# GpSimd forms the weights of hop 1's late sums, and a group of sums stands behind every stage of its last softmax

## The chip, the cores and the metric

The kernel runs on one core of one Trainium2 chip. The metric is the device time of one execution in microseconds; of a kernel the median of its runs counts.

## What is computed

A graph network with three hops over 25,000 edges, sorted by their head node, and 50,000 nodes of 128 numbers. Cut to what matters:

```python
h = maximum(layernorm(x), 0)                # 50000 x 128
agg = h
for _ in range(3):
    hd, t = agg[head], agg[tail]            # 25000 x 128
    att = sum((hd @ q_w) * tanh((rel * t) @ k_w), axis=1)
    w = softmax of att over the edges with the same head
    summed = segment_sum(w[:, None] * rel * t, head)
    agg = summed / max(count(head), 1)
    agg = agg / max(norm(agg), 1e-12)
    out = out + agg + h
result = x + out
```

## The kernel before, in words

The edges lie in 200 tiles of 125; four tiles make a group, 50 groups in all, and these fall into four chunks of 13, 13, 13 and 11 groups (`GC`). A hop goes over the groups in steps. In each step GpSimd has gathered the tail rows (L611), VectorE multiplies them with the relations (L1109), TensorE turns them (L1407), multiplies with the two matrices (L1414, L1427 or L1429), ScalarE takes the tanh (L1258), and VectorE forms the scores (L1133).

When all scores of a chunk are there, its **softmax** runs in eight stages (`softmax`, L961). VectorE and TensorE take turns: VectorE scans along rows and asks (`ask`), TensorE transposes (L1445, L1388, L1389, L1394, L1400) and answers. Stage 3 hands the differences to ScalarE for the exponential. Stage 7 leaves the weights of the chunk's edges in `wcol`, and `wfl` with the edges that belong to segments running over the end of a tile.

A **group of sums** (`sums`, L1079 on VectorE, L1471 on TensorE, L1279 on ScalarE) is this chain. VectorE forms four tiles of weights, `wr = (segbc == lcol) * wcol`, one instruction of 128x125 per tile (`weights`, L1040, L1047), in a ring of two groups: a group may be formed when TensorE has finished the group before the last (`s_T`). TensorE multiplies each with the tile's rows into one of two PSUM banks (L1478), once ScalarE has emptied that bank (`s_nr`). ScalarE forms the squares' sums (L1289) and copies the group back to `rt` (L1291). After VectorE has formed the weights of group j, it scales group j - 6 (`scale`, L1067), and at every fifth group first forms the scales of five groups from the squares' sums (`norms`, L1055 to L1062, twelve small instructions). SP then stores the scaled group (L506).

A segment that runs over a tile's end needs carries. TensorE forms two **partial sums** per tile (`parts`, L1461), VectorE scans them (`carries`, L1017), TensorE turns the result (L1468), VectorE copies it to `fxr` (L1038), and SP moves it into two rows of `rt` (L491). The first group of the next chunk waits for that (`s_cy`).

Most groups of the first three chunks are summed within the steps of the hop (`sums_by_step`). Those left over come after the last step, and this is where the change lies. In hop 1 these are groups 28 to 38 (`sums_left`), with the last chunk's softmax, its partial sums and its own groups 39 to 49. The order before, in hop 1:

- stages 0 to 4, with one of groups 28 to 32 behind each (`FILL = 5`, `sum_behind`); then stages 5, 6, 7 with none
- the 44 tiles of partial sums of the last chunk in four lots of 11, with one of groups 33 to 36 behind each (`sums_mixed`, `parts_left`)
- the carries, then groups 37 and 38 (`HOLD = 2`), then 39 to 49

After that come the last scales and stores. GpSimd's first gather of hop 2 waits for all stores of hop 1 (`s_cs`). In hops 0 and 2, 25 groups are left over.

Each engine works its queue in order, so an instruction of the softmax that stands behind a group of sums on TensorE waits for that group's weights too.

GpSimd's queue is: the gathers of hop 0 (L611), the scatter of its sums (L623), the 200 gathers of hop 1, the wait for hop 1's stores, the 200 gathers of hop 2, the scatter to the output. Its waits go through a helper (`pool_wait`, L594) that also counts up a semaphore of its own.

Of the kernel before, what the change touches and what calls it, by code (L numbers as in the profile page):

```python
# [9 lines left out]
ALU = mybir.AluOpType  # L10
# [4 lines left out]
R = 125  # L15
# [4 lines left out]
GT = 4  # L20
NG = NT // GT
# [4 lines left out]
K = 4  # L26
GC = [0, 13, 26, 39, NG]
# [90 lines left out]

FILL, HOLD = 5, 2

def sums_left(h):
    return range(SUMS[h][-1].stop, GC[LAST])

def sums_mixed(h):
    return sums_left(h)[FILL:len(sums_left(h)) - HOLD]

def sums_held(h):
# [2 lines left out]

def sum_behind(h, i):

    return sums_left(h)[i:i + 1] if i < FILL else range(0)

def parts_left(h, j):

    mixed = sums_mixed(h)
    each = -(-CT[LAST] // len(mixed))
    n = j - mixed.start
    return range(min(n * each, CT[LAST]), min((n + 1) * each, CT[LAST]))

def gnn_kernel(nc, x, src, dst, etype, edge_emb, q_w, k_w, out):
    ctx = ExitStack()  # L150
    with ctx:
        def sb(name, shape, dt=F32):
            return ctx.enter_context(nc.sbuf_tensor(name, shape, dt))

        def sem(name):
            return ctx.enter_context(nc.semaphore(name))
# [16 lines left out]
        segbc = sb("segbc", [P, NT, R], U8)  # L173
# [6 lines left out]
        wr = sb("wr", [P, 2 * GT, D])  # L180
# [26 lines left out]
        lcol = sb("lcol", [P, NT])  # L207
# [8 lines left out]
        wcol = sb("wcol", [P, NT])  # L216
# [114 lines left out]
        s_wf = sem("s_wf")  # L331
# [23 lines left out]
        s_w = sem("s_w")  # L355
        s_T = sem("s_T")
# [234 lines left out]
        def _(pool):  # L591
            G = nc.gpsimd

            def pool_wait(sem_, value):  # L594
                pool.wait_ge(sem_, value)
                pool.sem_inc(s_pace, 1)
# [13 lines left out]
            def fetch(row, n, table, idx, done):  # L610
                G.indirect_dma_start(out=row, out_offset=None, in_=table[:, :],  # L611
                                     in_offset=bass.IndirectOffsetOnAxis(ap=idx[:, n:n + 1], axis=0)).then_inc(done, 16)
# [39 lines left out]
            for g in range(NG):  # L652
                if g >= TS:
                    pool_wait(s_rt, NG + g - TS + 1)
                for t in range(GT):
                    fetch(tr[:, (g % TS) * GT + t, :], g * GT + t, ntab_d, tidx, s_t[g % TS])

            pool_wait(s_cs, 2 * 16 * NG)
            for g in range(NG):  # L660
# [12 lines left out]
        def _(dve):  # L673
# [366 lines left out]
            def weights(h, j):  # L1040
                if h == 0 and j == 0:
                    dve.wait_ge(s_bc, 16)
                if j >= 2:
                    dve.wait_ge(s_T, h * NG + j - 1)
                for t in range(GT):
                    n = j * GT + t
                    ins = V.tensor_scalar(wr[:, (j % 2) * GT + t, 0:R], segbc[:, n, :], lcol[:, n:n + 1], wcol[:, n:n + 1],  # L1047
                                          ALU.is_equal, ALU.mult)
                ins.then_inc(s_w, 1)

            def norms(h, i):

                dve.wait_ge(s_nr, h * NG + NB * (i + 1))
                v, y, a, z = (nwt[0:R, k, :] for k in range(4))
                ch(V.tensor_scalar(v, ssq[0:R, i % 2, :], 1e-30, None, ALU.max))  # L1055
                ch(V.tensor_scalar(y.bitcast(I32), v.bitcast(I32), -0.5, RSQRT_BITS, ALU.mult, ALU.add))
                for k in range(3):
                    ch(V.scalar_tensor_tensor(a, y, -0.5, y, ALU.mult, ALU.mult))
                    ch(V.tensor_tensor(a, a, v, ALU.mult))
                    ch(V.scalar_tensor_tensor(z, a, 1.5, y, ALU.add, ALU.mult))  # L1060
                    y, z = z, y
                ch(V.scalar_tensor_tensor(nsc[0:R, :], y, 1e12, invc[0:R, i * NB * GT:(i + 1) * NB * GT], ALU.min, ALU.mult))  # L1062

            def scale(h, j):
                u = j % NB
                if h < HOPS - 1:
                    V.tensor_tensor(edge_rows(j)[0:R], edge_rows(j)[0:R],  # L1067
                                    nsc[0:R, u * GT:(u + 1) * GT].unsqueeze(2).to_broadcast([R, GT, D]), ALU.mult).then_inc(s_ag, 1)
                    return
                dve.wait_ge(s_fl[j % 2], 48 * (j // 2 + 1))  # L1070
                for t in range(GT):
                    n = j * GT + t
                    ch.note(V.scalar_tensor_tensor(rt[0:R, n, 0:D], rt[0:R, n, 0:D], nsc[0:R, u * GT + t:u * GT + t + 1],  # L1073
                                                   base_in[j % 2][0:R, t, :], ALU.mult, ALU.add))
                ch.join()
                ch(V.tensor_tensor(edge_rows(j)[0:R], edge_rows(j)[0:R], one_in[j % 2][0:R], ALU.add))  # L1076
                V.tensor_tensor(edge_rows(j)[0:R], edge_rows(j)[0:R], two_in[j % 2][0:R], ALU.add).then_inc(s_ag, 1)

            def sums(h, j):  # L1079
                weights(h, j)  # L1080
                if j >= LAG:
                    if (j - LAG) % NB == 0:
                        norms(h, (j - LAG) // NB)
                    scale(h, j - LAG)
# [56 lines left out]
            for h in range(HOPS):  # L1141
                for s in range(STEPS[h]):
                    if h == 0:
# [14 lines left out]
                        for i, g in enumerate(unit):  # L1158
                            dve.wait_ge(s_t[g % TS], t_value(0, g))
                            for t in range(GT):  # L1160
                                j = (g % TS) * GT + t
# [33 lines left out]
                for j in sums_mixed(h):  # L1195
                    sums(h, j)
# [357 lines left out]
```

## Time and profile before

| what | value |
|---|---|
| median of 3 runs | 1969.43 us (1954.67 to 1972.27) |
| profiled execution | 1960.66 us, span 1958.8 us |
| granted TensorE clock, mean | 0.698 |
| PE busy | 1080.3 us (55%) |
| DVE busy | 1314.4 us (67%) |
| ACT busy | 859.3 us (44%) |
| POOL busy | 1260.1 us (64%) |
| weights on DVE (L1047), 600 instructions | 168.4 us |
| PE idle before L1478, ended by those weights | 111.0 us |

### The profile page before, as it was taken

How to read it: one execution, taken by the hardware profiler on the slowest of the kernel's cores; microseconds unless marked ns; L12 is line 12 of the kernel's file. 1: busy time of each engine (PE TensorE's matmuls, PEld its weight loads, DVE VectorE, ACT ScalarE, POOL GpSimd, SP SyncE). 2: the span in 40 equal slices, each digit the busy share in tenths (PEclk: the TensorE clock that was granted, in tenths of full speed). 3: DMA queues.
4: the chain of work that ended last, by engine and by line, in shares of the span. 5: the costliest groups of instructions: out<-in, count | busy, mean ns of one | idle time of the engine just before them, and what ended most of it. 6: DMA issues, size and time to landing. Idle time of an engine off the chain costs nothing. (4 is left out here: it accounts for less than half of the span.)

```text
span 1958.8 us, 23309 instructions
## 1 busy us (share of the span) xinstructions
PE 1080.3 (55%) x5196; PEld 861.5 (44%) x5196; DVE 1314.4 (67%) x5817; ACT 859.3 (44%) x2657; POOL 1260.1 (64%) x1218
## 2 busy tenths in 40 slices
PE   0112454458678587940016688787366886956410
PEld 0102333337456465930014567577244674746410
DVE  8896788786676675789813556865535458599870
ACT  3331666666564644656622243553422233234420
POOL 1005777667777777778777777700277777667776
PEclk9999866565676665565557887985677888655555
DMA  8925555554433334346745555621477789567761
GB/s 228 247 62 192 176 183 180 174 169 150 120 100 108 112 115 154 131 145 220 255 147 139 159 150 153 182 87 56 134 152 157 152 169 179 136 173 217 216 190 34
DMA packets 196490, 303.96 MB, mean 155 GB/s; under 512 B 31344, under 2 KB 113596, under 8 KB 189824
## 3 DMA queue, kind: packets, MB, share of 16 engines
q1 hardware_dynamic: 157952, 229.50, 36.6%
q0 software_dynamic: 38400, 72.99, 17.9%
q8 instruction: 42, 0.69, 0.1%
q14 instruction: 96, 0.79, 0.1%
HBM read 176.41 MB, written 131.38 MB: 157 GB/s over the span
## 5 line engine op out<-in xcount | busy, mean ns | idle before, releaser
L611 POOL DMA_INDIRECT tr<-in_x_dram,tidx x200 | 213.8, 1069 | 233.3 <-DVEq L845 152.1
L1478 PE MATMUL ps<-rt,wr 128*125 128x128 f32 x1200 | 256.6, 382 | 128.7 <-DVE wr L1047 111.0
L611 POOL DMA_INDIRECT tr<-agg_d,tidx x200 | 199.0, 995 | 191.0 <-issue 189.8
L1407 PE MATMUL ps<-ident,rt 128*128 128x128 f32 x600 | 133.7, 363 | 295.0 <-DVE rt L1109 177.8
L1478 PEld LDWEIGHTS ps<-rt,wr 128*125 128x125 f32 x1200 | 223.8, 278 | 148.7 <-DVE wr L1047 130.1
L1289 ACT ACTIVATE sqj<-ps,invc 125x128 bf16<-125x128 f32 x600 | 212.4, 374 | 171.3 <-PE ps L1478 171.3
L1252 ACT COPY turns<-ps 128x512 f32<-128x512 f32 x150 | 87.7, 585 | 411.5 <-PE ps L1407 407.1
L623 POOL DMA_INDIRECT ntab_d<-rt,lidx x200 | 224.0, 1120 | 63.9 <-issue 60.2
L623 POOL DMA_INDIRECT out_dram<-rt,lidx x200 | 211.3, 1056 | 73.6 <-issue 59.7
L611 POOL DMA_INDIRECT tr<-ntab_d,tidx x200 | 201.8, 1009 | 67.1 <-issue 62.6
L611 POOL DMA_INDIRECT xr<-in_x_dram,hidx x200 | 202.7, 1013 | 61.0 <-issue 59.5
L1414 PE MATMUL ps<-turns,kw 128*128 128x512 f32 x300 | 235.9, 881 | 8.7 <-ACT turns L1252 8.7
L1407 PEld LDWEIGHTS ps<-ident,rt 128*128 128x128 f32 x600 | 92.2, 186 | 322.1 <-DVE rt L1109 197.4
L1109 DVE TENSOR_TENSOR rt<-tr,relr 128x512 f32<-128x512 f32 x150 | 103.1, 688 | 147.7 <-DMA tr<-agg_d,tidx 86.7
L1461 PEld LDWEIGHTS ps<-wfl,rt 128*128 128x128 f32 x1200 | 189.9, 249 | 0.5
L1461 PE MATMUL ps<-wfl,rt 128*128 128x2 f32 x1200 | 186.0, 287 | 0.0
L1047 DVE TENSOR_SCALAR wr<-segbc,lcol,wcol 128x125 f32<-128x125 uint8 x600 | 168.4, 356 | 21.7 <-PE ps L1478 17.7
L1258 ACT ACTIVATE turns<-ps 128x512 f32<-128x512 f32 x150 | 89.6, 597 | 134.6 <-PE ps L1414 134.4
L1427 PEld LDWEIGHTS ps<-qwT,turns 128*128 128x128 f32 x624 | 107.2, 240 | 56.6 <-issue 55.0
L1289 ACT ACTIVATION_READ_ACCUMULATOR sqj<-ps,invc 125x1 f32 x600 | 127.9, 213 | 0.0
L1429 PEld LDWEIGHTS ps<-qwT,turns 128*128 128x128 f32 x576 | 99.2, 255 | 49.5 <-issue 40.6
L1133 DVE SCALAR_TENSOR_TENSOR junk<-ps,xr 128x128 bf16<-128x128 f32 x400 | 96.5, 282 | 25.2 <-PE ps L1429 24.2
(234 smaller groups left out, 2225.2 us busy)
## 6 DMA issues: line engine op xcount, KB each, us to landing
agg_d<-rt SPq DMA_DIRECT2D x100, 258.0 KB
xr<-agg_d SPq DMA_DIRECT2D x100, 258.0 KB, 3.3
relr<-rel_d SPq DMA_DIRECT2D x100, 256.0 KB, 3.9
ntab_d<-rt SPq DMA_DIRECT2D x15, 1679.7 KB
rt<-in_x_dram SPq DMA_DIRECT2D x13, 1024.0 KB, 6.7
out_dram<-rt SPq DMA_DIRECT2D x13, 1024.0 KB, 4.1
acc_d<-xr SPq DMA_DIRECT2D x50, 258.0 KB, 3.5
rel_d<-relr SPq DMA_DIRECT2D x50, 256.0 KB, 3.2
```

Of the source, the lines that this page charges most:

```text
L611: G.indirect_dma_start(out=row, out_offset=None, in_=table[:, :], in_offset=bass.IndirectOffsetOnAxis(ap=idx[:, n:n + 1], axis=0)).then_in ...
L623: G.indirect_dma_start(out=table[:, :], out_offset=bass.IndirectOffsetOnAxis(ap=lidx[:, n:n + 1], axis=0), in_=rt[:, n, 0:width], in_offse ...
L1047: ins = V.tensor_scalar(wr[:, (j % 2) * GT + t, 0:R], segbc[:, n, :], lcol[:, n:n + 1], wcol[:, n:n + 1], ALU.is_equal, ALU.mult)
L1109: V.tensor_tensor(edge_rows(g), ring(tr, g, TS), ring(relr, g, RS), ALU.mult).then_inc(s_rt, 1)
L1133: ins = V.scalar_tensor_tensor(junk[:, t, :], z, 1.0, left[:, (g % n) * GT + t, 0:D], ALU.mult, ALU.mult, accum_out=att[:, g * GT + t:g * ...
L1289: A.activation(sqj[0:R, t, :], ps[B_T + j % 2][0:R, t, :], ACT.Square, scale=invc[0:R, n:n + 1], accum_out=ssq[0:R, j // NB % 2, k:k + 1]) ...
L1407: ins = T.transpose(ps[B_TR][:, t, :], rt[:, g * GT + t, 0:D], ident[:, :])
L1414: T.matmul(bank(B_KW), kw[:, :], flat2(rtT[:, (g % 2) * GT:(g % 2 + 1) * GT, :]), start=True, stop=True).then_inc(s_rg, 1)
L1427: ins = T.matmul(z, th, qwT[:, :], start=True, stop=True)
L1429: ins = T.matmul(ps[B_Z + g % 2][:, t, :], th, qwT[:, 0:D], start=True, stop=True)
L1461: ins = T.matmul(bank(B_S)[:, 2 * n:2 * n + 2], rt[:, TC[b] + n, 0:D], wfl[:, n, :], start=True, stop=True)
L1478: ins = T.matmul(ps[B_T + j % 2][0:R, t, :], wr[:, (j % 2) * GT + t, 0:R], rt[:, j * GT + t, 0:D], start=True, stop=True)
```

## The change

In hop 1, from group 28 on, GpSimd forms the weights (22 groups, 88 instructions), and VectorE leaves them out. `FILL` becomes a list: in hop 1 there is now a group of sums behind each of the eight stages (28 to 35). That leaves one group, 36, among the partial sums, so all 44 stand in one block ahead of it. Groups 37 to 49 are as before. Hops 0 and 2 keep their order, and their weights stay on VectorE.

```diff
-FILL, HOLD = 5, 2
+FILL, HOLD = [5, 8, 5], 2
...
 def sums_mixed(h):
-    return sums_left(h)[FILL:len(sums_left(h)) - HOLD]
+    return sums_left(h)[FILL[h]:len(sums_left(h)) - HOLD]
...
 def sum_behind(h, i):
-    return sums_left(h)[i:i + 1] if i < FILL else range(0)
+    return sums_left(h)[i:i + 1] if i < FILL[h] else range(0)
+
+
+def by_pool(h, j):
+
+    return h == 1 and j >= sums_left(h)[0]
...
             for g in range(NG):
                 if g >= TS:
                     pool_wait(s_rt, NG + g - TS + 1)
                 for t in range(GT):
                     fetch(tr[:, (g % TS) * GT + t, :], g * GT + t, ntab_d, tidx, s_t[g % TS])
 
+            pool_wait(s_w, NG + sums_left(1)[0])
+            for j in range(sums_left(1)[0], NG):
+                if j == sums_left(1)[0] or j in GC:
+                    pool_wait(s_wf, K + 1 + max(c for c in range(K) if GC[c] <= j))
+                pool_wait(s_T, NG + j - 1)
+                for t in range(GT):
+                    n = j * GT + t
+                    ins = G.tensor_scalar(wr[:, (j % 2) * GT + t, 0:R], segbc[:, n, :], lcol[:, n:n + 1], wcol[:, n:n + 1],
+                                          ALU.is_equal, ALU.mult)
+                ins.then_inc(s_w, 1)
+
             pool_wait(s_cs, 2 * 16 * NG)
...
             def sums(h, j):
-                weights(h, j)
+                if not by_pool(h, j):
+                    weights(h, j)
                 if j >= LAG:
```

`s_wf` counts the chunks whose softmax is done, and `s_w` the groups of weights formed.

TensorE, hop 1, from stage 5 to the carries, before (L1394 is stage 5, L1400 stage 6, L1461 the partial sums, L1478 groups of sums, x4 each):

```order
L1394 MATMUL ps<-ident,rcar 44x1 x2
L1400 MATMUL ps<-ident,wlin 128x44
L1459 MATMUL ps<-cell,onesr 128x1
L1461 MATMUL ps<-wfl,rt 128x2 x11
L1478 MATMUL ps<-rt,wr 125x128 x4
L1461 MATMUL ps<-wfl,rt 128x2 x11
L1478 MATMUL ps<-rt,wr 125x128 x4
L1461 MATMUL ps<-wfl,rt 128x2 x11
L1478 MATMUL ps<-rt,wr 125x128 x4
L1461 MATMUL ps<-wfl,rt 128x2 x11
L1478 MATMUL ps<-rt,wr 125x128 x4
L1468 MATMUL ps<-ident,cT 44x128 x2
```

The same stretch now (L1412 is stage 5, L1418 stage 6, L1479 the partial sums, L1496 groups of sums):

```order
L1412 MATMUL ps<-ident,rcar 44x1 x2
L1496 MATMUL ps<-rt,wr 125x128 x4
L1418 MATMUL ps<-ident,wlin 128x44
L1496 MATMUL ps<-rt,wr 125x128 x8
L1477 MATMUL ps<-cell,onesr 128x1
L1479 MATMUL ps<-wfl,rt 128x2 x44
L1496 MATMUL ps<-rt,wr 125x128 x4
L1486 MATMUL ps<-ident,cT 44x128 x2
```

Three groups of sums have moved ahead: one behind stage 5, and two (x8) behind stage 6 and stage 7, which gives TensorE nothing to do. The 44 tiles of partial sums stand together, with one group between them and the carries' transposes (L1486).

VectorE, hop 1, from the carries' copy (L1038) on, before (L1047 weights, L1067 the scaling of a group, L1055 to L1062 the scales of five groups):

```order
L1038 COPY fxr<-ps 44x256
L1047 TENSOR_SCALAR wr<-segbc,lcol,wcol 128x125 x4
L1067 TENSOR_TENSOR rt<-rt,nsc 125x4x128
L1047 TENSOR_SCALAR wr<-segbc,lcol,wcol 128x125 x4
L1067 TENSOR_TENSOR rt<-rt,nsc 125x4x128
L1047 TENSOR_SCALAR wr<-segbc,lcol,wcol 128x125 x4
L1067 TENSOR_TENSOR rt<-rt,nsc 125x4x128
L1047 TENSOR_SCALAR wr<-segbc,lcol,wcol 128x125 x4
L1067 TENSOR_TENSOR rt<-rt,nsc 125x4x128
L1047 TENSOR_SCALAR wr<-segbc,lcol,wcol 128x125 x4
L1055 TENSOR_SCALAR nwt<-ssq 125x20
L1056 TENSOR_SCALAR nwt<-nwt 125x20
```

The same place now (L1055 the copy, L1084 the scaling, L1072 on the scales):

```order
L1055 COPY fxr<-ps 44x256
L1084 TENSOR_TENSOR rt<-rt,nsc 125x4x128 x4
L1072 TENSOR_SCALAR nwt<-ssq 125x20
L1073 TENSOR_SCALAR nwt<-nwt 125x20
L1075 SCALAR_TENSOR_TENSOR nwt<-nwt 125x20
L1076 TENSOR_TENSOR nwt<-nwt 125x20
```

The weights of groups 37 to 41 are gone from between the scalings. GpSimd's queue shows where they went; before:

```order
L623 DMA ntab_d<-rt,lidx 50000x129 x32
L616 IOTA rt 128x100
L623 DMA ntab_d<-rt,lidx 50000x129 x168
L611 DMA tr<-ntab_d,tidx 128x129 x200
L611 DMA tr<-agg_d,tidx 128x129 x200
L623 DMA out_dram<-rt,lidx 50000x128 x200
```

and now:

```order
L629 DMA ntab_d<-rt,lidx 50000x129 x32
L622 IOTA rt 128x100
L629 DMA ntab_d<-rt,lidx 50000x129 x168
L617 DMA tr<-ntab_d,tidx 128x129 x200
L671 TENSOR_SCALAR wr<-segbc,lcol,wcol 128x125 x88
L617 DMA tr<-agg_d,tidx 128x129 x200
L629 DMA out_dram<-rt,lidx 50000x128 x200
```

The 88 instructions stand between the last gather of hop 1 (L617) and the first of hop 2. No other engine's queue has anything added; ScalarE and SP keep their order.

## Rows read from the trace of the kernel before

**Rows 1.** windows: stages, partial sums, tail and end of hop 1

```profile
core 0: us, PE busy (x) PEld busy (x) DVE busy (x) ACT busy (x) POOL busy (x), PEclk, DMA share, GB/s
1313.10:1335.40 22.30, 12.22 (x53) 9.71 (x51) 19.28 (x80) 12.12 (x56) 0.00 (x0) 0.50 0.18 70
1335.40:1362.30 26.90, 26.88 (x124) 26.34 (x124) 9.76 (x38) 6.33 (x30) 0.00 (x0) 0.50 0.11 40
1362.30:1396.30 34.00, 20.39 (x104) 18.32 (x104) 26.79 (x91) 26.50 (x125) 0.00 (x0) 0.74 0.29 111
1396.30:1406.10 9.80, 2.03 (x8) 1.86 (x8) 6.20 (x23) 0.02 (x1) 0.00 (x0) 0.55 0.37 136
```

**Rows 2.** chain that ended last, same part: start us, us, what

```profile
1313.21 1.11 DVE wr L1047 x4
...
1327.94 1.12 DVE wr L1047 x4
...
1335.41 0.58 PE ps L1459 x2
1335.99 4.79 PE ps L1461 x22
1340.78 1.91 PE ps L1478 x8
...
1361.87 0.44 PE ps L1468 x2
...
1362.75 1.03 DVE wr L1047 x4
```

**Rows 3.** timeline of the stages: start us, us, engine, line, [idle before <-releaser]

```profile
1314.38 2.07 PE L1478 MATMUL ps<-rt,wr 128*125 128x128 f32 x8 [0.60 <-DVE wr L1047]
...
1331.37 0.15 DVE L934 TENSOR_TENSOR seg_xf<-seg_x,ps 44x1 f32<-44x1 f32 x1 [1.05 <-PE ps L1394]
...
1334.43 0.33 PE L1400 MATMUL ps<-ident,wlin 44*128 44x44 f32 x1 [3.10 <-DVEq L820]
```

**Rows 4.** timeline of the tail of hop 1

```profile
1376.44 3.69 PE L1478 MATMUL ps<-rt,wr 128*125 128x128 f32 x16 [3.09 <-DVE wr L1047]
...
1378.29 0.37 ACT L1289 ACTIVATE sqj<-ps,invc 125x128 bf16<-125x128 f32 x1 [2.44 <-PE ps L1478]
...
1390.48 0.37 ACT L1289 ACTIVATE sqj<-ps,invc 125x128 bf16<-125x128 f32 x1 [2.69 <-PE ps L1478]
...
1396.36 0.18 DVE L1055 TENSOR_SCALAR nwt<-ssq 125x20 f32<-125x20 f32 x1 [3.56 <-ACT rt L1291]
```

**Rows 5.** chain, tail and end of hop 1: squares, copy, store

```profile
1365.93 1.50 ACT sqj L1289 x8
1367.43 0.48 ACT rt L1291
...
1402.03 3.01 DMA agg_d<-rt
```

**Rows 6.** timeline, carries of chunk 2: from their copy to the sum behind them

```profile
1302.71 0.42 DVE L1038 COPY fxr<-ps 52x256 f32<-52x256 f32 x1 [2.27 <-PE ps L1468]
...
1307.11 0.95 PEld L1478 LDWEIGHTS ps<-rt,wr 128*125 128x125 f32 x8 [0.22 <-DMA rt<-fxr]
```

**Rows 7.** groups on POOL: xcount | busy us, mean ns | idle before

```profile
L611 POOL DMA_INDIRECT tr<-agg_d,tidx x200 | 199.0, 995 | 191.0 <-issue 189.8 <-DVE rt L1109 1.2
L604 POOL IOTA rt<- 128x256 f32 x7 | 5.0, 739 | 0.0
...
L616 POOL IOTA rt<- 128x100 f32 x2 | 0.7, 373 | 0.0
L601 POOL TENSOR_SCALAR_AFFINE_SELECT ident<-ident 128x128 f32<-128x128 f32 x1 | 0.3, 292 | 0.1
```

**Rows 8.** groups by form, 1286 to 1402 us, scaling on DVE

```profile
L1067 DVE TENSOR_TENSOR rt<-rt,nsc 125x512 f32<-125x512 f32 x32 | 21.5, 684 | 0.2
```

**Rows 9.** chain in hop 2: 26 instructions of partial sums

```profile
1598.70 2.80 PE ps L1461 x26
```

## The prediction

> **What bounds the kernel now.** I read the page first (no engine is busy for the whole span), then the chain that ended last, then the waits and the timeline of the one place that the change touches: the last part of hop 1, from the moment the last scores are formed (1313.1 us) to the first gather of hop 2 (1406.1). Everything of hop 2 waits for the stores at its end, so what this part gives is given to the span. The windows [rows 1] cut it in four. In all of them GpSimd has 0.00 to 0.02 us of work.
>
> - Stages, 22.3 us. The last softmax is a ladder between VectorE and TensorE. Five of its eight stages have a group of sums behind them, and the chain runs over the four weights of each on VectorE, 1.11 us per group (first and last of five in [rows 2]). TensorE is busy for 12.22 of 22.30 us at a granted clock of 0.50, which is its 1.2 GHz level. It stood idle for 0.60 us for the first weights and for 3.10 us ahead of stage 6's transpose; VectorE waited 1.05 us behind a group of sums [rows 3].
> - Partial sums, 26.9 us: TensorE is full (26.88) and the chain stays on it [rows 1, 2]: 22 instructions of partial sums, a group of sums at 1.91 us, four times over.
> - Tail, 34.0 us, thirteen groups (37 to 49). ScalarE does 26.50 us of work, VectorE 26.79. After every five groups VectorE forms the scales, and weights stand in its queue behind that; TensorE then stands for 3.09 us for weights, and ScalarE for 2.44 and 2.69 us [rows 4].
> - End: scales, five groups scaled, the last store of 3.01 us [rows 5].
>
> **The change, part by part.** The sum is made against the profiled execution, 1960.66 us (span 1958.8); the median of the runs shown is 1969.43, so that execution lies 8.8 us below it.
>
> *The weights leave VectorE.* 22 groups (28 to 49), 88 instructions, about 1.1 us a group, 24 us of VectorE's time. The same 88 go to GpSimd, which has nothing to do there, behind the 200 gathers of hop 1 and ahead of the wait for the stores, and that wait ends later anyway. The trace has none of these on GpSimd, so their price is bounded. From below: of the ops it does show, the affine_select over 128 elements took 0.292 us, the iotas 0.373 for 100 elements and 0.739 for 256, that is 2.35 ns per element and 0.14 us fixed [rows 7]; 125 elements would be 0.43 by that. The far upper end is the one other GpSimd instruction, the gather's, at 0.995. I take 0.4 (between the two near rows), 1.6 us a group; with a wait ahead of it, some 1.8.
>
> *What stands in GpSimd's way.* Before each group it waits until TensorE has finished the group before the last (two buffers of weights). A buffer's round is then 1.8 + 2.07 (TensorE, low clock, [rows 3]) + 0.2 that I allow for signalling = 4.1 us for two groups, 2.03 each. ScalarE needs 1.50 + 0.48 [rows 5] and 0.12 that I allow between groups, 2.1 each. So GpSimd is just not the bound, at 0.4 us an instruction. Behind its waits nothing else is queued until the gathers of hop 2.
>
> *Stages.* I walked the ladder with the weights ready in time and TensorE at its low clock. TensorE's queue keeps its order, so each stage's transposes come behind a 2.07 us group. Group 28 then runs from 1313.8 (1314.38 in [rows 3]), 29 from 1316.2, 30 and 31 from 1318.6 to 1322.7, 32 from 1325.3 (ahead of it VectorE forms the scales of five groups, as before), 33 to 1329.8. Stage 6 is asked at about 1330.6 instead of 1334.4, since the weights no longer lie between the stages. Group 34 runs to 1333.1 and 35 to 1335.2; VectorE is done with stage 7 by 1332. TensorE has room: 12.22 + 3 x 2.07 = 18.4 of 22.3 us. The partial sums then start where they do now, 1335.4. Cost of three more groups in the stages: 0. If that cover failed wholly it would be 6.2.
>
> *Partial sums.* Three of the four groups between them are gone to the stages: 3 x 1.91 = 5.7 us less, and 44 partial sums in one block keep their 18.2 us (the stretch from 1335.99 to 1361.87 less four groups of 1.91). TensorE comes to the carries' transposes at 1356.1 instead of 1361.87. **Gain 5.7.**
>
> *Tail.* Group 37's weights no longer wait for the carries' copy on VectorE (1362.75 in [rows 2]), and there is no stall at the scales. What is late next is ScalarE: 2.1 us for the first group on TensorE, 13 x 2.1 = 27.3, and 0.6 because group 39 needs the carries' rows landed: copy to sum took 4.4 us in [rows 6], while TensorE would get there 0.6 sooner. Together 30.0 instead of 34.0. **Gain 4.0.** The end (last scales, five groups scaled, store) is the same.
>
> *A shared port.* In this stretch GpSimd and VectorE never worked at once [rows 1], so no row shows what they do to each other. Some 20 instructions of the ladder have two inputs in SBUF, and so has each scaling, 0.684 us [rows 8]. Bounds: 0, and a full GpSimd instruction of 0.4 ahead of each of the 20, 8 us. GpSimd is at work about two thirds of the time and a wait is on average half an instruction, but in the stages TensorE's groups cover most of it. I take **1.2 lost**. (The Trainium skill, SBUF — State Buffer, section Who interferes with whom, speaks against the change here: a VectorE instruction with two SBUF inputs and a GpSimd instruction that reads SBUF exclude each other, and the later one blocks fully. By it the term is above zero; no run here shows it yet.)
>
> Sum: 5.7 + 4.0 - 1.2 = 8.5 us. 1960.66 - 8.5 = 1952.2; from the median, 1969.43 - 8.5 = **1960.9 us**, 0.4% less.
>
> **Rivals.**
>
> *A. GpSimd just becomes the bound.* With 0.7 us an instruction a group takes 2.8 us, more than ScalarE's 2.1. Group 28's weights, begun once VectorE has formed group 27's (before the 1313.21 of [rows 2]), stand at about 1314.4, as now [rows 3]; group 35's, seven times 2.8 later, at 1334, so the stages end a microsecond later. The block of partial sums gives its 5.7. In the tail group 38's weights wait for group 36, and eleven groups at 2.8 eat most of the gain: in all about 2 us faster, 1967.4. For it: the iota's row at 256 elements costs 0.739. Against: 125 elements are half of that. (The Trainium skill, GPSIMD Engine Reference, section Elementwise — side-by-side cycle accounting, gives about 2.6 cycles an element against VectorE's one, and calls it roughly twice as slow; 125 elements at 2.6 cycles of 1.2 GHz is 0.27 us before dispatch, an estimate. Twice VectorE's time would be this rival.)
>
> *B. GpSimd is far too slow (slower than before).* At 1.0 us an instruction, the gather's price, a group needs 4.2 us with its wait. TensorE's queue holds each stage's transposes behind a group without weights: group 35's weights stand at 1345 (28's at 1315.8, then seven times 4.2), so the partial sums start at 1347 instead of 1335.4; they and group 36 end at 1368; groups 38 to 49 then come every 4.2 us, and ScalarE ends at about 1422 instead of 1396.3. That is 26 us slower, 1995. It decides from about 0.72 us an instruction (slower at all), and passes 1% from about 0.93. For it: nothing on this engine shows float compare and multiply from bytes. Against: its near rows are all under 0.43 at this size.
>
> *C. TensorE's clock rises.* The stages and the partial sums run at 0.50 now [rows 1]; in the tail it is 0.74. With groups back to back in the stages it may stand at its 2.4 GHz level when the partial sums start. At that level 26 instructions took 2.80 us [rows 9], 44 partial sums (88 instructions) 9.5 instead of 18.2: 8.7 more, and up to 2 in the stages. Gain 17 to 19, 1951. For it: after a run of groups without a gap the tail's clock rises. Against: TensorE was full from 1335.4 to 1362.3 and its clock still stayed at 0.50, so partial sums alone do not raise it, nor perhaps hold it.
>
> *D. The stages give nothing back*, since the ladder itself gets longer by what leaves the partial sums: gain about 3, 1966.
>
> **Chances.** Forecast 0.52, A 0.14, B 0.10, C 0.16, D 0.08. The runs before spread from 1954.67 to 1972.27, so about 1% (20 us) is what a measurement can tell from no change. Range: C below with some spread, 1946; above, A and D with the spread of a median, and part of B, 1975; B's own time is left out with its 0.10. The forecast's own range is 1953 to 1968. Faster by over 1% needs C and luck: 0.13. Slower by over 1% is most of B: 0.08. Within: 0.79.
>
> **What would show it.** Right: 88 instructions of weights on GpSimd near 0.4 us each; the block of partial sums starting within 1.5 us of where it did and 18 us long; TensorE not waiting for GpSimd in the tail, ScalarE's groups 2.1 us apart; the carries 5 to 6 us sooner; first gather of hop 2 near 1397 to 1398 us. Wrong: TensorE's waits named after GpSimd's weights and groups further apart than 2.3 us (A, B); a granted clock above 0.6 in the partial sums (C); partial sums that start after 1338 (D); VectorE's scaling well over 0.684 us (the port's term); or a hop 2 whose length is not that of before by more than 3 us, where nothing is changed.

## The result and the profile after

| kernel | median | profiled execution | span |
|---|---|---|---|
| before | 1967.43 us (20 runs, 1954.67 to 1973.32) | 1960.66 us | 1958.8 us |
| after | 1978.7 us (20 runs, 1965.23 to 1994.05) | 1978.9 us | 1977.0 us |

The ratio is 1.0063, 95% interval 1.0043 to 1.0082: about 12.4 us slower. The forecast was 8.5 us faster, 1960.9, and its range ended at 1975.

Both traces are cut at the same five events: the transposes of the last scores, the first matmul of the partial sums' block, the carries' transposes, the end of ScalarE's last copy, and the first gather of hop 2.

| section, us | before | after | difference |
|---|---|---|---|
| stages of the last softmax | 22.05 | 29.40 | +7.35 |
| partial sums | 26.25 | 21.15 | -5.10 |
| tail | 34.66 | 47.50 | +12.84 |
| end | 9.80 | 9.60 | -0.20 |
| sum | 92.77 | 107.65 | +14.88 |

After came to the first event 2.1 us earlier (1311.28 against 1313.36), so its first gather of hop 2 stands at 1418.92 instead of 1406.12: 12.8 us later, close to the 12.4 of the ratio. The two spans differ by 5.4 us more, in hop 2, where nothing is changed; that part varied by more than 10 us between the executions below. Of the profiled executions below, those of experiments 2, 3 and 4 are over 1.5% longer than the fastest of the same kernel, so only their sections are compared, which repeat where nothing in them was changed.

The windows of after, cut like [rows 1] (us; PE, PEld, DVE, ACT and POOL busy with their instructions; granted clock; DMA share and GB/s):

```profile
core 0: us, PE busy (x) PEld busy (x) DVE busy (x) ACT busy (x) POOL busy (x), PEclk, DMA share, GB/s
1311.30:1340.70 29.40, 18.10 (x76) 14.84 (x74) 18.81 (x68) 16.26 (x74) 29.40 (x34) 0.50 0.20 78
1340.70:1361.80 21.10, 21.10 (x99) 21.06 (x99) 3.10 (x14) 1.98 (x9) 4.62 (x6) 0.50 0.04 13
1361.80:1409.30 47.50, 26.83 (x108) 22.90 (x105) 14.72 (x39) 27.74 (x126) 42.94 (x48) 0.54 0.21 80
1409.30:1418.90 9.60, 2.03 (x8) 1.86 (x8) 6.21 (x23) 0.02 (x1) 0.00 (x0) 0.50 0.37 138
```

POOL is busy for 29.40 of 29.40 us in the stages and for 42.94 of 47.50 in the tail. It is the engine that had nothing to do here before. VectorE, which the change was to relieve, is down to 14.72 us in the tail, and ScalarE, which the forecast saw as the next bound, works 27.74 of 47.50. The waits of after from 1300 to 1430 us (who waits <- for what: us in all, times, longest) say the same in one row each:

```profile
ACT sqj L1307 <- PE ps L1496: 54.3, 22, 19.3
...
DVE nwt L1072 <- ACT rt L1309: 35.0, 4, 10.9
PEld ps L1496 <- POOL wr L671: 32.7, 19, 3.7
PE ps L1496 <- POOL wr L671: 27.7, 19, 3.4
...
PE ps L1496 <- DVE wr L1064: 4.1, 2, 2.5
```

TensorE waited 19 times for GpSimd's weights, 27.7 us in all. The 54.3 us of ScalarE behind TensorE (39.9 in the same stretch before) are in part the same shortage one engine further on; a wait names only the engine just ahead. The timeline of the stages, which answers to [rows 3] (idle time and its releaser in brackets), shows how regular it is:

```profile
1313.99 2.07 PE L1496 MATMUL ps<-rt,wr 128*125 128x128 f32 x8 [2.29 <-POOL wr L671]
...
1317.29 2.07 PE L1496 MATMUL ps<-rt,wr 128*125 128x128 f32 x8 [1.00 <-POOL wr L671]
...
1324.21 2.07 PE L1496 MATMUL ps<-rt,wr 128*125 128x128 f32 x8 [1.03 <-POOL wr L671]
...
1328.33 2.07 PE L1496 MATMUL ps<-rt,wr 128*125 128x128 f32 x8 [1.14 <-POOL wr L671]
...
1338.68 2.07 PE L1496 MATMUL ps<-rt,wr 128*125 128x128 f32 x8 [1.40 <-POOL wr L671]
...
1341.19 18.93 PE L1479 MATMUL ps<-wfl,rt 128*128 128x2 f32 x88
```

Before, TensorE stood for 0.30 to 1.41 us for VectorE's weights ahead of each of five groups, 4.05 in all. Now it stands for GpSimd's ahead of each of eight, 2.29 at group 28 and 0.94 to 1.59 at the others, 10.4 in all, and the partial sums (last row) begin 29.9 us after the first event instead of 22.6. The tail, for [rows 4]:

```profile
1362.84 2.48 DVE L1084 TENSOR_TENSOR rt<-rt,nsc 125x512 f32<-125x512 f32 x4
...
1367.58 1.72 PE L1496 MATMUL ps<-rt,wr 128*125 128x128 f32 x8 [3.42 <-POOL wr L671]
...
1381.77 2.07 PE L1496 MATMUL ps<-rt,wr 128*125 128x128 f32 x8 [2.83 <-POOL wr L671]
...
1384.86 2.07 PE L1496 MATMUL ps<-rt,wr 128*125 128x128 f32 x8 [1.02 <-POOL wr L671]
...
1387.95 2.07 PE L1496 MATMUL ps<-rt,wr 128*125 128x128 f32 x8 [1.02 <-POOL wr L671]
...
1399.04 2.07 PE L1496 MATMUL ps<-rt,wr 128*125 128x128 f32 x8 [2.78 <-POOL wr L671]
...
1409.35 0.18 DVE L1072 TENSOR_SCALAR nwt<-ssq 125x20 f32<-125x20 f32 x1 [10.95 <-ACT rt L1309]
```

From the group at 1384.86 to that at 1387.95 it is 3.09 us: GpSimd's own pace, four instructions. The longer idle times (3.42, 2.83, 2.78) stand at groups 38, 42 and 47. 12 steps of 3.09, and 2.2, 1.8 and 1.8 more at the three long ones, make 42.9 us; the rest of 47.5 is 0.4 ahead of the first step and 4.2 for TensorE's and ScalarE's work on the last group.

The price of one instruction, which [rows 7] could only bound, is now a row of the page (xcount | busy, mean ns | idle before):

```profile
L671 POOL TENSOR_SCALAR wr<-segbc,lcol,wcol 128x125 f32<-128x125 uint8 x88 | 77.9, 900 | 53.5 <-DVE wr L1064 36.6
```

and by the view of that line alone (ns, least/median/most):

```profile
L671 POOL TENSOR_SCALAR wr<-segbc,lcol,wcol x88: 785/789/2969, 1310.3 to 1404.4; 128x125 f32<-128x125 uint8 x88
```

The median is 0.789 us where I took 0.4. The mean of 0.900 and the longest of 2.969 show a second thing, taken up below.

### The profile page after: what moved, and what is told of

It is laid out like the page before. It is cut to its first block and busy times, and to the rows that moved or that the text cites. A ratio compares the mean times of both kernels' runs of the same rounds, so it can differ in the third digit from the quotient of the medians.

```text
span 1977.0 us, 23334 instructions
## 1 busy us (share of the span) xinstructions
PE 1084.8 (55%) x5196; PEld 865.4 (44%) x5196; DVE 1295.4 (66%) x5729; ACT 861.3 (44%) x2657; POOL 1331.5 (67%) x1306
## 5 line engine op out<-in xcount | busy, mean ns | idle before, releaser
L617 POOL DMA_INDIRECT tr<-in_x_dram,tidx x200 | 211.3, 1057 | 230.9 <-DVEq L862 152.0
L1496 PE MATMUL ps<-rt,wr 128*125 128x128 f32 x1200 | 263.7, 389 | 139.7 <-DVE wr L1064 98.6
L1496 PEld LDWEIGHTS ps<-rt,wr 128*125 128x125 f32 x1200 | 228.9, 284 | 161.2 <-DVE wr L1064 110.8
L617 POOL DMA_INDIRECT tr<-ntab_d,tidx x200 | 200.2, 1001 | 72.9 <-issue 65.8
L617 POOL DMA_INDIRECT tr<-agg_d,tidx x200 | 197.4, 987 | 74.4 <-issue 59.8
L617 POOL DMA_INDIRECT xr<-in_x_dram,hidx x200 | 204.3, 1022 | 61.0 <-issue 59.4
L1479 PEld LDWEIGHTS ps<-wfl,rt 128*128 128x128 f32 x1200 | 188.4, 248 | 0.5
L1479 PE MATMUL ps<-wfl,rt 128*128 128x2 f32 x1200 | 185.4, 287 | 0.0
L1064 DVE TENSOR_SCALAR wr<-segbc,lcol,wcol 128x125 f32<-128x125 uint8 x512 | 143.8, 362 | 11.3 <-PE ps L1496 7.9
L671 POOL TENSOR_SCALAR wr<-segbc,lcol,wcol 128x125 f32<-128x125 uint8 x88 | 77.9, 900 | 53.5 <-DVE wr L1064 36.6
```

The costliest lines, as they stand in the source:

```text
L1479: ins = T.matmul(bank(B_S)[:, 2 * n:2 * n + 2], rt[:, TC[b] + n, 0:D], wfl[:, n, :], start=True, stop=True)
L1496: ins = T.matmul(ps[B_T + j % 2][0:R, t, :], wr[:, (j % 2) * GT + t, 0:R], rt[:, j * GT + t, 0:D], start=True, stop=True)
```

## The experiments

All are compared by the sections above. The sections hold no wait for a large transfer, and they came out alike where nothing in them was changed: the partial sums took 21.15 us in nine of the kernels below, and 26.25 in the three that keep their old order. The timing of a whole execution says less: it moves by several us in hop 2. The first four ran on a chip on which the kernel before itself took 2519.87 us, and transfers were slower there (119 to 123 GB/s over the span in these four profiles instead of 157); their ratios are 0.997 [0.989, 1.005], 0.999 [0.989, 1.009], 0.994 [0.986, 1.002] and 0.987 [0.978, 0.997]. These don't decide between theories a few us apart. The last of them even lies below 1 while its four sections are 1.2 us longer; what gave that kernel its time elsewhere is open.

| us | stages | partial sums | tail | end | sum |
|---|---|---|---|---|---|
| before | 22.05 | 26.25 | 34.66 | 9.80 | 92.77 |
| after | 29.40 | 21.15 | 47.50 | 9.60 | 107.65 |
| 1. order alone | 27.25 | 21.15 | 34.59 | 9.85 | 92.84 |
| 2. GpSimd alone, old order | 23.57 | 26.25 | 47.62 | 9.32 | 106.75 |
| 3. 32 columns | 22.74 | 21.15 | 34.35 | 9.28 | 87.54 |
| 4. GpSimd in the stages alone | 29.19 | 21.15 | 34.45 | 9.21 | 94.00 |
| 5. four columns | 21.88 | 18.04 | 31.09 | 9.07 | 80.08 |
| 6. constants | 23.57 | 21.15 | 36.88 | 9.10 | 90.70 |
| 7. short scalings | 27.16 | 21.15 | 43.07 | 9.13 | 100.52 |
| 8. seven groups on GpSimd | 24.20 | 21.15 | 30.33 | 9.14 | 84.82 |
| 9. three groups, old order | 22.10 | 26.25 | 28.75 | 9.25 | 86.35 |
| 10. 32 columns, short scalings | 20.59 | 21.15 | 28.43 | 8.81 | 78.97 |
| 11. float input | 29.13 | 21.15 | 47.43 | 9.56 | 107.28 |

Two theories stood at the start. GpSimd's price: an instruction costs about 0.79 us and nothing else matters much. Against it the order: eight groups among the stages hold the softmax up whoever forms their weights.

**1. The order alone.** VectorE forms all weights again, in the new order.

```diff
 def by_pool(h, j):
-    return h == 1 and j >= sums_left(h)[0]
+    return False
```

> The new order of groups alone: a group behind each of the eight stages, and all weights on VectorE. Theory 1 (the loss comes from GpSimd's 0.79 us an instruction, the order is sound): the stretch from the last score to the partial sums grows by 3 to 5 us against the kernel before (22.9 us there), the partial sums and group 36 take 20.3 us up to the carries' transposes instead of 26.3, the tail stays at 34 us; in all 1 to 3 us less than before, ratio about 0.999. Theory 2 (the order itself costs what the partial sums give, rival D): the stages grow by 6 us or more, ratio 1.000 to 1.002.

The result lies between the two theories: the stages grew by 5.2, and nothing is gained in all. The sum is that of before, 92.84 against 92.77. What leaves the partial sums (5.1 us) comes back in the stages (5.2): the ladder gets longer by VectorE's weights for three more groups. The tail is unchanged. Its timeline in the stages (this chip's times lie later; L1485 groups of sums, L1407 the transpose of stage 6):

```profile
1725.13 2.07 PE L1485 MATMUL ps<-rt,wr 128*125 128x128 f32 x8 [0.84 <-DVE wr L1053]
...
1742.77 0.33 PE L1407 MATMUL ps<-ident,wlin 44*128 44x44 f32 x1 [1.44 <-DVEq L826]
...
1743.97 4.16 PE L1485 MATMUL ps<-rt,wr 128*125 128x128 f32 x16 [0.87 <-DVE wr L1053]
```

TensorE waits for weights ahead of the groups (0.84, 0.87 us) and for VectorE's request ahead of the transpose (1.44 us): VectorE has both to do, one after the other, and the request comes later for each group of weights ahead of it. So the order alone is worth nothing, and costs nothing either. Of after's 7.35 us in the stages, 5.2 are there with VectorE's weights too, and GpSimd adds 2.15.

**2. GpSimd alone.** The old order, GpSimd's weights.

```diff
-FILL, HOLD = [5, 8, 5], 2
+FILL, HOLD = [5, 5, 5], 2
```

> The weights of hop 1 from group 28 on by GpSimd, in the old order (five stages with a group, four lots of partial sums). Theory 1: the tail is as long as in the changed kernel, 46 to 48 us instead of 34, since GpSimd forms a group in 3.1 us and more where a scaling of VectorE blocks it; the stages grow by 2 to 4 us; the lots of partial sums hide GpSimd. In all 14 to 17 us more than before, ratio about 1.008, a little worse than the changed kernel's 1.0063. Theory 2: ratio at or below 1.004, since three groups less in the stages wait for GpSimd.

The tail is as long as after's (47.62), the partial sums are as before, and the stages, with five groups instead of eight, take 23.57. The loss in the tail is GpSimd's alone. In the stages GpSimd alone costs 1.5 us (2 to 4 were expected), the order alone 5.2, and both together 7.35. The sum is 14.0 us longer than before, as expected; the ratio can't tell it on that chip.

**3. A shorter instruction.** GpSimd forms 32 of the 125 columns.

```diff
-G.tensor_scalar(wr[:, (j % 2) * GT + t, 0:R], segbc[:, n, :], ...
+G.tensor_scalar(wr[:, (j % 2) * GT + t, 0:32], segbc[:, n, 0:32], ...
```

> The changed kernel with GpSimd's instructions cut to 32 of 125 columns, so 93 columns of each tile's weights in hop 1 from group 28 on are left as they were and the sums there are not the reference's. This tells whether GpSimd's price is the one term that failed. Theory 1: an instruction falls to 0.2 to 0.35 us, GpSimd is no longer waited for, the partial sums start about where they do in the kernel before, the tail takes 29 to 31 us instead of 34: 6 to 10 us less than before, ratio 0.995 to 0.997, which is the forecast. Theory 2 (the price of an instruction is mostly fixed): it stays above 0.6 us and the ratio above 1.002. Theory 3 (my walk of the stages or the tail was wrong too): GpSimd is fast and the ratio still at 0.999 or above.

```profile
L671 POOL TENSOR_SCALAR wr<-segbc,lcol,wcol x88: 463/470/2975, 1749.3 to 1824.2; 128x32 f32<-128x32 uint8 x88
```

The median of 0.470 us lies between the first two theories (0.2 to 0.35, and over 0.6). At it the order does what the forecast said of it: 22.74 us of stages with eight groups, and the 5.1 us of the partial sums kept. But the tail is still 34.35, not 29 to 31. Four instructions at 0.47 are 1.9 us a group, no more than ScalarE needs, so a second cost was left in it: the longest instruction still took 2.975 us.

**4. GpSimd for groups 28 to 36 alone.**

```diff
-    return h == 1 and j >= sums_left(h)[0]
+    return h == 1 and sums_left(h)[0] <= j < 37
```

> The changed kernel with GpSimd for groups 28 to 36 alone; from group 37 on VectorE forms the weights as before. Theory 1: the tail goes back to 33 to 35 us and only the stages' loss against the partial sums' gain is left, about +2 us: ratio 1.000 to 1.002. Rival: the tail stays long (over 40 us), so that something else than the weights' maker lengthens it.

The tail goes back to 34.45, the stages stay at 29.19. Each loss is there without the other: 7.1 us here, 13.0 in the tail of experiment 2.

**5, 6, 11. What the price is made of.** Four columns instead of 125; constants in place of the two columns of scalars; a float tile (`ident`) as input in place of bytes.

```diff
-... segbc[:, n, :], lcol[:, n:n + 1], wcol[:, n:n + 1], ...
+... segbc[:, n, 0:4], lcol[:, n:n + 1], wcol[:, n:n + 1], ...   (5, output 0:4)
+... segbc[:, n, :], 3.0, 0.5, ...                               (6)
+... ident[:, 0:R], lcol[:, n:n + 1], wcol[:, n:n + 1], ...      (11)
```

> The changed kernel with GpSimd's instructions cut to 4 of 125 columns (121 columns of each tile's weights from group 28 of hop 1 on are left as they were). From 125 columns (0.773 us from start to start) and 32 columns (0.447) a line gives 0.335 us fixed and 3.5 ns a column. Theory: 0.35 us here. If it is 0.30 or less or 0.40 or more, the line does not hold and part of the price has another shape (steps, or a floor).

> The changed kernel with constants (3.0 and 0.5) in place of the two columns lcol and wcol that GpSimd's instruction reads per partition, so the sums from group 28 of hop 1 on are not the reference's. With 125 columns an instruction took 0.79 us and with 32 columns 0.60 on average, so the price is mostly fixed. Theory 1: the fixed part is the reading of the two scalar columns; then an instruction falls to 0.4 us or less, and the tail from 47.5 to about 34. Theory 2: the fixed part belongs to the instruction itself; then it stays at 0.7 us or more and the tail at 45 us or more.

> The changed kernel with GpSimd's instruction reading 125 float columns (the identity matrix) instead of 125 bytes of segbc, so the sums from group 28 of hop 1 on are not the reference's. Theory 1 (the 3.5 ns a column are the reading of bytes and their conversion): an instruction falls from 0.773 us, start to start, to 0.65 or less. Theory 2 (they are the two operations a column): it stays within 0.03 of 0.773, and the sections keep their lengths of 29.4, 21.2 and 47.5 us.

The same line of each trace, first with four columns:

```profile
L671 POOL TENSOR_SCALAR wr<-segbc,lcol,wcol x88: 372/378/2969, 1318.1 to 1386.5; 128x4 f32<-128x4 uint8 x88
```

with constants:

```profile
L671 POOL TENSOR_SCALAR wr<-segbc x88: 635/638/2991, 1314.2 to 1392.2; 128x125 f32<-128x125 uint8 x88
```

with float input:

```profile
L671 POOL TENSOR_SCALAR wr<-ident,lcol,wcol x88: 786/788/2968, 1309.1 to 1403.0; 128x125 f32<-128x125 f32 x88
```

From one start to the next, in a stretch without a wait, it is 0.773 us for 125 columns, 0.447 for 32 and 0.360 for 4. A line through the first two has 3.5 ns a column and 0.335 us fixed, and gives 0.349 for the third. Constants make it 0.606, between the two theories of experiment 6, and the tail 36.88. So the two columns of scalars cost 0.167 us of an instruction of 125 columns; whether that is fixed or grows with the columns no run shows. Bytes or floats make no difference (789 and 788). VectorE starts one of these every 0.254 us, four in 1.02, so GpSimd is 3.0 times as slow in this one. (The Trainium skill, GPSIMD Engine Reference, section Elementwise — side-by-side cycle accounting, has about 2.6 cycles an element and a ratio of 1.96, for an add of two tensors. This instruction, with one tensor and two columns of scalars, is dearer in the trace: 3.5 ns is 4.2 cycles at that section's 1.2 GHz, and the ratio is 3.0.)

**7. The shared port.** VectorE's scalings are cut to one of their four tiles (125x128 in place of 125x512) from group 22 on; they last 0.31 us on the mean instead of 0.72. The weights are full size.

```diff
+if h == 1 and j >= 22:
+    V.tensor_tensor(edge_rows(j)[0:R, 0:1], edge_rows(j)[0:R, 0:1], ...
+    return
```

> The changed kernel with VectorE's scaling cut to one of four tiles from group 22 of hop 1 on, so three quarters of those rows stay unscaled. It takes away most of the time in which VectorE reads two inputs in SBUF. Theory 1 (that is what stretches GpSimd's instructions beyond 0.79 us: 2.97 us for the one that meets four scalings in a row, 1.39 for each of three that meet a row of five): the longest falls below 1.3 us, the mean from 0.90 to about 0.82, and the tail from 47.5 to 43 or 44 us. Rival: the long ones stay, and the mean stays at 0.88 or more; then they belong to GpSimd itself.

```profile
L671 POOL TENSOR_SCALAR wr<-segbc,lcol,wcol x88: 786/789/1370, 1307.3 to 1394.7; 128x125 f32<-128x125 uint8 x88
```

The longest instruction falls from 2.969 to 1.370 us (below 1.3 was expected), the tail by 4.4 and the stages by 2.2. In the tail VectorE is idle most of the time, so its own shorter work cannot give that; it is what the scalings did to GpSimd. The 1.370 stands beside a row of four short scalings, so part of the cost is still there, and 4.4 is the least that the port takes in the tail. In the stages part of the 2.2 may be VectorE's own time. How it happens stands in after's timeline: the tail's first row above is four scalings back to back from 1362.84, 2.48 us. The GpSimd instruction that began at 1363.02, in the first of them, ended at 1365.98, 0.67 us behind the last. The two later sets of five scales free five scalings each, and GpSimd's group of that moment took 4.9 us instead of 3.1. There GpSimd wasn't kept out for the whole row: its instructions took 1.39 us three times at 1377.57, and 1.91 and 1.39 at 1395.70. VectorE pays less; by after's groups of 1286 to 1409 us:

```profile
L1084 DVE TENSOR_TENSOR rt<-rt,nsc 125x512 f32<-125x512 f32 x27 | 18.6, 719 | 1.0
...
L1077 DVE SCALAR_TENSOR_TENSOR nwt<-nwt 125x20 f32<-125x20 f32 x15 | 3.5, 234 | 0.5
```

The scaling is at 719 ns on the mean against 684 in [rows 8]. That mean mixes two kinds: 19 of the 27 took 674 to 694 ns, among them the four that kept GpSimd out, and eight took 760 to 934. The small instruction of the scales, L1077, is at 234 against 178 for the same one before. (The Trainium skill, SBUF — State Buffer, section Who interferes with whom, says that the two exclude each other and the later one is blocked fully. For GpSimd at 1363.02 the trace agrees, 2.97 us. For VectorE it doesn't agree: no scaling was held for as much as half of a GpSimd instruction, and the last section has VectorE instructions that ran at their own length inside one.)

**10. Both at once.** Edits 3 and 7 together: a lower price, and less of the port.

> 32 of 125 columns in GpSimd's instructions and VectorE's scaling cut to one of four tiles from group 22 of hop 1 on (93 columns of the weights are left as they were, three quarters of the rows unscaled). With 32 columns alone the tail took 34.4 us although a group cost GpSimd only 1.8 us. Theory (three runs of scalings, each of which holds one GpSimd instruction for 2 to 3 us, make that tail): the tail falls to 28 to 30 us, the end by 2 us since the scalings are short, and no GpSimd instruction is longer than 1.4 us. Rival (the walk of the tail is wrong, ScalarE and TensorE need more than 2.1 us a group between them): the tail stays at 32 us or more.

```profile
L671 POOL TENSOR_SCALAR wr<-segbc,lcol,wcol x88: 466/474/1377, 1312.4 to 1379.3; 128x32 f32<-128x32 uint8 x88
```

Its windows (stages, partial sums, tail):

```profile
1313.60:1334.10 20.50, 14.40 (x75) 12.02 (x73) 13.43 (x61) 15.82 (x74) 17.47 (x34) 0.75 0.28 107
1334.10:1355.30 21.20, 21.20 (x100) 21.09 (x100) 3.49 (x19) 2.05 (x10) 1.93 (x5) 0.50 0.04 13
1355.30:1383.70 28.40, 18.34 (x107) 15.80 (x105) 8.08 (x39) 26.76 (x126) 23.52 (x48) 0.80 0.36 133
```

20.59 and 28.43 us. Against experiment 3 the tail gives 5.9, so the port is the second cost there too. The stages give 2.15, but TensorE's granted clock in them is 0.75 here and 0.58 in experiment 3, so that part can be the clock's. The end fell by 1.0 us to 8.81 where 2 were expected. ScalarE is now busy for 26.76 of 28.40 us in the tail: the bound that the forecast named. This and experiment 3 leave most of the weights unformed, so they tell what the rest of the kernel allows and are no kernels to use. One timed run each: 1948.66 us for this, 1954.86 for four columns, 1984.11 for float input, beside 1977.74 for the kernel before; 1965.58 for constants and 1970.89 for short scalings, beside 1966.73.

**8 and 9. Give GpSimd what it has time for.** If 3.1 to 4.9 us is the price of a group, GpSimd can do one in several, ahead of time, in buffers of its own, while VectorE does the others. In 8 that is seven groups in the new order, in 9 three in the old one: 37, 42 and 47, those that stood right behind the scales of five groups on VectorE.

```diff
+PG = [29, 31, 33, 35, 37, 42, 47]      # 9: [37, 42, 47] and FILL 5
 def by_pool(h, j):
-    return h == 1 and j >= sums_left(h)[0]
+    return h == 1 and j in PG
...
+for i, j in enumerate(PG):
+    if i > 1:
+        pool_wait(s_T, NG + PG[i - 2] + 1)
+    ... wp[:, (i % 2) * GT + t, 0:R] ...
+    ins.then_inc(s_wp, 1)
```

> A version to beat both: the new order with a group behind each stage, GpSimd forming only groups 29, 31, 33, 35, 37, 42 and 47 of hop 1, in two buffers of its own (the idle one-hot buffer), VectorE the others. 3.2 us a group then has two groups' time in the stages, and the three in the tail are those that stand behind VectorE's five-group scales. Theory 1: stages 24 to 26 us, partial sums 21, tail 29.5 to 31.5 us (ScalarE's 2.1 a group), last score to first gather 84 to 87.5 us instead of 92.8, ratio about 0.997. Rival (VectorE itself is the bound in the tail): the tail stays at 33 us or more.

> The order of the kernel before, with GpSimd forming only groups 37, 42 and 47 of hop 1 in buffers of its own. Theory 1: stages 22.1 and partial sums 26.2 us as before, tail 29.5 to 31.5 instead of 34.7, ratio about 0.998. Rival: the tail stays at 33 us or more since VectorE's own work, 26.8 us of 34, and the exchange with ScalarE set it and not the weights behind the scales.

Windows of 8:

```profile
1318.10:1342.30 24.20, 14.76 (x76) 12.20 (x74) 22.02 (x82) 15.63 (x74) 10.71 (x12) 0.71 0.23 87
1342.30:1363.40 21.10, 21.10 (x99) 21.05 (x99) 4.17 (x19) 2.23 (x10) 3.17 (x4) 0.50 0.05 19
1363.40:1393.70 30.30, 21.07 (x108) 18.07 (x105) 23.67 (x79) 26.97 (x126) 5.17 (x4) 0.76 0.33 124
1393.70:1402.90 9.20, 2.03 (x8) 1.86 (x8) 6.21 (x23) 0.05 (x1) 0.01 (x1) 0.57 0.38 144
```

and of 9:

```profile
1315.90:1338.00 22.10, 12.01 (x52) 9.51 (x50) 19.18 (x80) 12.15 (x56) 0.00 (x0) 0.50 0.18 68
1338.00:1364.30 26.30, 26.26 (x123) 26.20 (x124) 9.85 (x38) 5.95 (x27) 4.36 (x4) 0.50 0.11 41
1364.30:1393.00 28.70, 17.76 (x107) 14.61 (x105) 23.74 (x79) 27.16 (x126) 5.86 (x4) 0.86 0.35 131
1393.00:1402.30 9.30, 2.03 (x8) 1.85 (x8) 6.21 (x23) 0.04 (x1) 0.01 (x1) 0.50 0.38 142
```

Both are faster than before, by little. 8: 1955.32 us (12 runs), ratio to before 0.9953 [0.9928, 0.9979]. 9: 1959.55 us (12 runs), 0.9963 [0.9933, 0.9993]. The intervals overlap and don't tell the two apart. By the sections they are 8.0 and 6.4 us shorter than before, 0.41% and 0.33%. POOL is busy for 5.17 and 5.86 us in the tail, where ScalarE is the bound (26.97 of 30.30, 27.16 of 28.70). Kernel 9, which moves three groups and keeps the order, takes 5.9 us off the tail; the seven of kernel 8 give 4.3 there and 5.1 in the partial sums, and pay 2.15 in the stages. What the buffers of their own give, and what the fewer groups, was not told apart. A combination (the new order with VectorE's scalings kept away from GpSimd's groups) was not tried.

## Why the prediction was wrong, by its steps

**The step that failed is the price of GpSimd's instruction, "I take 0.4".** It measured 0.79 at the median and 0.90 on the mean. The rows it was taken from were of other kinds: the iota reads nothing, and its line (0.14 us fixed, 2.35 ns an element) was short in both terms, against 0.335 and 3.5 here. The far bound of 0.995 held, and the truth lay nearer to it than to the two rows that I took for near. Nearness in shape (some 125 elements) was not nearness in kind (an input in SBUF and two columns of scalars).

**The shared port, 1.2 lost:** wrong in size and in form. Experiment 7 gives 6.7 us back (4.4 in the tail, 2.2 in the stages), within the bounds of 0 to 8; not the whole of it, since short scalings still hold GpSimd, and with some of VectorE's own time in it. I had priced the small instructions that wait for GpSimd. What cost was GpSimd held at rows of scalings, which the sum did not have.

**Stages, 0:** right for weights that come in time (22.74, 21.88 and 20.59 us in experiments 3, 5 and 10, against 22.05 before), wrong for those of after, +7.35. The text said that a failed cover would cost up to 6.2; the cover that failed was GpSimd's, which forms the eight groups in 28.3 us, 3.5 each, not TensorE's room (18.10 us busy, forecast 18.4). With VectorE's weights it fails too, by 5.2 (experiment 1).

**Partial sums, -5.7:** right, -5.10, at a clock of 0.50 as before; with the same block and other weights, experiments 1 and 3 have the same 21.15.

**Tail, -4.0 to 30.0:** the walk was right for its bound. With the bound really at ScalarE it took 28.43 (experiment 10), 28.75 (9) and 30.33 (8). With GpSimd at 3.1 us a group it took 47.50. **End, 0:** right, -0.20.

Put together, at the first gather of hop 2 the forecast was 21.3 us off (-8.5 against +12.8): 16.8 in the tail, 7.35 in the stages, 0.6 in the partial sums; less the 1.2 already taken for the port, the 2.1 of the earlier start and 0.2 at the end. Of the 24.2 in tail and stages experiment 7 gives 6.7 back; experiment 3, with the price at 0.47 and the scalings whole, gives 19.8 back, and both edits together 27.9, with a higher clock in the stages. So the price is the larger part; an exact split no run shows.

**Rivals.** B named what happened, with its place and its break-even: slower at all from 0.72 us, 1% slower from 0.93. Its own line (26 us at 1.0, nothing at 0.72) gives 5 us at 0.773 and 16 at 0.89, which is the pace in the tail with the port's share (42.9 us over 12 steps, a quarter of each); measured 12.8. It had a chance of 0.10 and was left out of the range. With a price bounded from 0.29 to 0.995 and a break-even at 0.72, nearly four tenths of those bounds lay beyond it, and the range should have reached some way into it. A was too mild: it put 0.7 on the near side. Its last sentence doesn't come out either: twice VectorE's 1.1 us a group is 2.2, 0.55 an instruction, which is near ScalarE's 2.1 a group and not A's 2.8. C did not happen in after (0.50 in stages and partial sums), but part of it is real. With four columns the three windows read:

```profile
1319.10:1340.90 21.80, 15.42 (x75) 13.08 (x73) 16.37 (x62) 15.52 (x74) 16.31 (x34) 0.66 0.27 104
1340.90:1359.00 18.10, 18.10 (x100) 17.98 (x100) 3.80 (x19) 2.31 (x10) 1.59 (x5) 0.59 0.04 16
1359.00:1390.10 31.10, 18.52 (x107) 16.07 (x105) 13.62 (x39) 27.09 (x126) 24.61 (x48) 0.83 0.33 121
```

The clock was granted at 0.66 in the stages and 0.59 in the partial sums, which took 18.04 us instead of 21.15. In experiment 10 it stood at 0.75 in the stages and 0.50 right behind them. D, the ladder that gets longer by what leaves the partial sums, is what experiment 1 shows, but with VectorE forming the weights, not GpSimd.

## What to carry to other kernels

Price an idle engine by an instruction of the same kind as the one it is to take, with the same inputs and scalars; if the trace has none, work out the price at which the change turns, and if that lies inside the bounds, let the range cross it. An engine three times as slow can still help if it takes one group in five, ahead of time and in buffers of its own, at the point where the faster engine is held up; given all of them, it becomes the bound of everything behind it. And look at what the relieved engine does next: its instructions back to back may be what holds the helper.

## What the runs showed of the hardware

- On GpSimd, a compare-and-multiply over 128 partitions with two columns of scalars costs 0.335 us plus 3.5 ns a column (start to start 0.773 us at 125 columns, 0.447 at 32, 0.360 at 4). With constants it is 0.606 at 125 columns. Byte or float input is the same, 789 and 788 ns.
- A row of VectorE instructions with two inputs in SBUF can hold one GpSimd instruction for the whole row: 2.97 us at four scalings of 2.48 us together, and the scalings kept their 0.68. At two rows of five it didn't: GpSimd's instructions took 1.39 us three times, or 1.91 and 1.39, and the scalings up to 0.77 and 0.83. What decides between the two was not tested.
- Which of the small VectorE instructions with two such inputs is held goes with the moment of its start. In after's timeline:

```profile
1322.31 0.18 DVE L1075 SCALAR_TENSOR_TENSOR nwt<-nwt 125x20 f32<-125x20 f32 x1
1322.53 0.18 DVE L1076 TENSOR_TENSOR nwt<-nwt 125x20 f32<-125x20 f32 x1
1322.74 0.32 DVE L1077 SCALAR_TENSOR_TENSOR nwt<-nwt 125x20 f32<-125x20 f32 x1
```

GpSimd's instructions began at 1321.82 and 1322.59 and took 0.79 us each. So L1075 ran at its own length inside the first, and L1077, begun 0.15 us into the second, took 0.14 us more. All six L1077 of the stages and the partial sums began 0.15 to 0.16 us into a GpSimd instruction and took 0.32 us; the six of the tail began 0.5 us or more into one and took 0.18. It isn't a rule without exception: at 1393.45 an L1075 began 0.15 us into one and took 0.18, and the GpSimd instruction took 0.84. The one-input L1073 was slower beside GpSimd too, 277 ns on the mean of five against 176 before, and why no run tells.
